# Maxima over adjacent queries, and a turned store of their negatives, in a cross-attention kernel

## The reference, cut to what matters

```
query = hidden @ Wq; keyt = enc @ Wk; valt = enc @ Wv       # 2 x 1024 queries, 2044 keys, width 640
hs = mha(query, keyt, valt)                                 # 8 heads of 80, softmax over the keys
ca_q1 = einsum('btc,th->bch', ca, Wq_ca)[:, indices, :]     # 4 tokens, 384 distinct rows
ca_hs1 = mha(ca_q1, hidden, hidden)
ca_hs2 = mha(ca_hs1 @ Wq, ca @ Wk_ca, ca @ Wv_ca)
out = (hs + ca_hs2) @ Wout + b_out + hidden
```

## Time and profile before

| what | value |
| --- | --- |
| median of the three executions | 1228.3 us |
| the profiled execution's own time | 1228.01 us |
| its span, first to last instruction | 1226.2 us |
| granted TensorE clock over the span | 1.00 |
| busy: PE, PEld | 1214.0 us, 956.8 us |
| busy: DVE, ACT, POOL | 829.0, 679.7, 205.6 us |
| PE, line 210 (maxima): count, busy | 480, 194.2 us |

### The profile page before, as it was taken

The page is one execution under the profiler, slowest core; times in us unless marked ns, Lnnn a source line. Parts: engine busy times, 40 slices in busy tenths (PEclk is TensorE's granted clock), DMA queues, the critical chain, the costliest instruction groups (busy, mean ns, idle before and its releaser), DMA issues.

```text
span 1226.2 us, 14526 instructions
## 1 busy us (share of the span) xinstructions
PE 1214.0 (99%) x5644; PEld 956.8 (78%) x5644; DVE 829.0 (68%) x1168; ACT 679.7 (55%) x773; POOL 205.6 (17%) x114
## 2 busy tenths in 40 slices
PE   7999999999999999999999999999999999999999
PEld 6889888898667677777777777777777777776899
DVE  6439825592244378888878878888888888885552
ACT  6333324222544367677677677677677677778310
POOL 1100000001000011312322222221221221221233
PEclk9999999999999999999999999999999999999999
DMA  8974795793840064154254344344345335332254
GB/s 304 350 284 165 237 344 199 265 315 94 234 115 1 1 194 97 65 151 109 80 137 108 91 126 108 104 119 111 105 112 127 95 103 146 111 91 65 69 211 150
DMA packets 80335, 180.68 MB, mean 147 GB/s; under 512 B 17305, under 2 KB 33945, under 8 KB 76138
## 3 DMA queue, kind: packets, MB, share of 16 engines
q1 hardware_dynamic: 72554, 157.33, 42.5%
q0 software_dynamic: 2816, 11.80, 3.0%
q10 hardware_dynamic: 4896, 10.62, 2.5%
HBM read 116.32 MB, written 63.24 MB: 146 GB/s over the span
## 4 chain that ended last, share of the span: by engine, by line
PE 99%; ACT 0%; DMA 0%; issue 0%; DVE 0%; ACTq 0%
PE at_ps L1232 29%; PE bank L653 20%; PE at_ps L1213 19%; PE at_ps L210 9%; PE acc_t_ps L1009 7%; PE at_ps L1419 6%; PE s_ps L976 2%; PE bank L630 2%; PE bank L600 1%; PE f_ps L949 1%; PE acc_t_ps L987 1%; PE f_ps L210 1%; PE f_ps L928 1%; PE f_ps L938 0%; DMA ctx_f<-in_ctxT 0%; PE at_ps L1422 0%
## 5 line engine op out<-in xcount | busy, mean ns | idle before, releaser
L218 DVE TENSOR_REDUCE mpart<-at_ps 128x1 f32<-128x512 f32 x480 | 326.7, 687 | 109.7 <-PE at_ps L210 108.1
L1154 ACT ACTIVATE prob_hi<-at_ps 128x1024 fp32r<-128x1024 f32 (+1 forms) x256 | 263.2, 1028 | 194.4 <-PE at_ps L1213 194.4
L1232 PE MATMUL at_ps<-prob_hi,v 128*81 128x512 f32 (+1 forms) x1024 | 318.9, 396 | 0.2 <-issue 0.2
L1091 DVE TENSOR_TENSOR prob_lo<-probs,prob_hi 128x1024 fp32r<-128x1024 f32 (+1 forms) x211 | 271.1, 1285 | 23.4 <-ACT probs L1159 23.4
L1159 ACT ACTIVATE probs<-at_ps 128x1024 f32<-128x1024 f32 (+1 forms) x256 | 261.1, 1020 | 0.0
L1232 PEld LDWEIGHTS at_ps<-prob_hi,v 128*81 128x81 f32 (+1 forms) x1024 | 153.8, 151 | 59.5 <-issue 6.1
L1091 POOL TENSOR_TENSOR prob_lo<-probs,prob_hi 128x1024 fp32r<-128x1024 f32 x45 | 108.1, 2402 | 519.7 <-ACT probs L1159 519.7
L210 PE MATMUL at_ps<-a 128*128 128x512 f32 x480 | 194.2, 405 | 0.0
L210 PEld LDWEIGHTS at_ps<-a 128*128 128x128 f32 x480 | 153.6, 320 | 32.0 <-DVE mpart L218 1.3
L1213 PE MATMUL at_ps<-a 128*128 128x512 f32 (+1 forms) x512 | 161.5, 396 | 1.2 <-ACT probs L1159 0.6
L1213 PE MATMUL at_ps<-b 113*128 113x512 f32 (+1 forms) x512 | 160.6, 394 | 0.0
(11 more groups left out here) (144 smaller groups left out, 1452.8 us busy)
## 6 DMA issues: line engine op xcount, KB each, us to landing
v_hi_d<-v_t SPq DMA_DIRECT2D x16, 648.0 KB, 6.4
v_lo_d<-v_t SPq DMA_DIRECT2D x16, 648.0 KB, 8.5
v<-v_hi_d SPq DMA_DIRECT2D x16, 648.0 KB, 4.8
v<-v_lo_d SPq DMA_DIRECT2D x16, 648.0 KB, 5.9
k_hi_d<-out_hi SPq DMA_DIRECT2D x40, 256.0 KB, 4.8
k_lo_d<-out_lo SPq DMA_DIRECT2D x40, 256.0 KB, 5.4
a<-k_hi_d SPq DMA_DIRECT2D x16, 640.0 KB, 7.3
b<-k_hi_d SPq DMA_DIRECT2D x16, 640.0 KB, 10.9
```

The costliest lines, as they stand in the source:

```text
L218: dve.tensor_reduce(self.mpart[:, g % 2, qt, c:c + 1], mx_ps[k % 2][:, 0:w], AX, ALU.max).then_inc(self.mx_done, 1)
L1091: eng.tensor_tensor(pl[n % PB][0:r, :], prob[n % PF][0:r, :], ph[n % PB][0:r, :].bitcast(F32), ALU.subtract).then_inc(sem, 1)
L1154: act.activation(ph[n % PB][0:r, :], s_ps[n % 2][0:r, :], ACT.Exp, scale=SCALE).then_inc(ph_done, 1)
L1232: mm = pe.matmul(o_ps[:, u * CH:(u + 1) * CH], a[0:r, t, :], y[n % PB][0:r, u * CH:(u + 1) * CH], start=t == 0 and m == 0, stop=t == KT - ...
```

## The change

The query tile of a step takes 128 adjacent queries, so its weights lie side by side. Partition p of the negated maxima then holds queries p, p+128, and so on. A thirty-third step per head turns them: PE multiplies the 128 x 8 negated maxima (as weights) with an identity of 128 x 128, which gives 8 rows of 128 in the PSUM buffer of the step; DVE copies them to `mrow`; SP stores the 8 rows as 8 runs of 512 bytes. `STEPS` is 33, and the buffers alternate over it. The identity is a new input, loaded once by SP in the token stage and copied once by POOL.

The new step stands in tile 12 of the head before (for head 0 in the token stage, one round behind step 31). PE has nothing between the scores there, then the new step, then the first two steps of the next head:

```diff
 NA = 3
 MXN = ST * SKV // CH
+STEPS = MXN + 1
 FIRST_PIECES = (2, 3, 2, 3, 3, 2, 3, 3, 2, 3, 3, 3)
 EARLY = 4
...
         self.mtop = sb("mtop", [P, 2, ST])
         self.mneg = sb("mneg", [P, 2, ST], F32R)
+        self.eye = sb("eye", [P, P], F32R)
+        self.mrow = sb("mrow", [ST, 2, P], F32R)
 
         self.qk_in = [sem(f"at_qk_in{r}") for r in range(NA)]
...
 
         p = g % 2
-        sp.wait_ge(self.neg_done, g + 1)
-        sp.dma_start(self.queries_b(g)[SHIFT:SHIFT + 1, :].rearrange("o (q g) -> o q g", q=P).bitcast(F32),
-                     self.mneg[:, p, :].bitcast(F32)).then_inc(self.neg_in[p], 16)
+        sp.wait_ge(self.mx_done, (g + 1) * STEPS)
+        sp.dma_start(self.queries_b(g)[SHIFT:SHIFT + 1, :].rearrange("o (t q) -> o t q", q=P).bitcast(F32),
+                     self.mrow[:, p, :].bitcast(F32)).then_inc(self.neg_in[p], 16)
 
     def score_piece(self, pe, mx_ps, g, k):
 
-        n = g * MXN + k
-        qt, c = divmod(k, SKV // CH)
-        w = min(CH, SK - c * CH)
+        n = g * STEPS + k
+        to = mx_ps[n % 2]
         if k == 0:
             self.a_loaded(pe, g)
         if n >= 2:
             pe.wait_ge(self.mx_done, n - 1)
-        pe.matmul(mx_ps[k % 2][:, 0:w], self.queries_a(g)[:, qt:SQ:ST], self.keys_a(g)[:, c * CH:c * CH + w],
-                  start=True, stop=True).then_inc(self.mx_full, 1)
+        if k < MXN:
+            qt, c = divmod(k, SKV // CH)
+            w = min(CH, SK - c * CH)
+            pe.matmul(to[:, 0:w], self.queries_a(g)[:, qt * P:(qt + 1) * P], self.keys_a(g)[:, c * CH:c * CH + w],
+                      start=True, stop=True).then_inc(self.mx_full, 1)
+        else:
+            if g == 0:
+                pe.wait_ge(self.eye_done, 1)
+            pe.wait_ge(self.neg_done, g + 1)
+            pe.matmul(to[0:ST, 0:P], self.mneg[:, g % 2, :], self.eye[:], start=True, stop=True
+                      ).then_inc(self.mx_full, 1)
 
     def max_piece(self, dve, mx_ps, g, k):
-        n = g * MXN + k
-        qt, c = divmod(k, SKV // CH)
-        w = min(CH, SK - c * CH)
+        n = g * STEPS + k
+        at = mx_ps[n % 2]
         dve.wait_ge(self.mx_full, n + 1)
-        dve.tensor_reduce(self.mpart[:, g % 2, qt, c:c + 1], mx_ps[k % 2][:, 0:w], AX, ALU.max
-                          ).then_inc(self.mx_done, 1)
+        if k < MXN:
+            qt, c = divmod(k, SKV // CH)
+            w = min(CH, SK - c * CH)
+            dve.tensor_reduce(self.mpart[:, g % 2, qt, c:c + 1], at[:, 0:w], AX, ALU.max).then_inc(self.mx_done, 1)
+        else:
+            dve.tensor_copy(self.mrow[:, g % 2, :], at[0:ST, 0:P]).then_inc(self.mx_done, 1)
 
     def top(self, dve, g):
 
         p = g % 2
-        dve.wait_ge(self.mx_done, (g + 1) * MXN)
+        dve.wait_ge(self.mx_done, g * STEPS + MXN)
         dve.tensor_reduce(self.mtop[:, p, :], self.mpart[:, p], AX, ALU.max).then_inc(self.mtop_done, 1)
         dve.wait_ge(self.mtop_done, g + 1)
...
         onehot_f = ca_f[:, 0:SQ]
         onehot = s.sb("onehot", [P, SQ], F32R)
+        eye_f = s.sb("eye_f", [P, P])
         p1 = [kept["p1_0"]] + [s.sb(f"p1_{i}", [P, 2, CD]) for i in (1, 2)]
         raw = kept["raw"]
...
 
             k -= MAX_FROM * pairs
-            return [k] if 0 <= k < MXN else []
+            return [k] if 0 <= k < STEPS else []
 
         def folded(n):
...
             written(sp)
             sp.dma_start(kept["wk2"][:], d["wk2_frame"]).then_inc(wk2_in, 16)
+            sp.dma_start(eye_f[:], d["eye"]).then_inc(eye_in, 16)
             shift_tokens(sp, kept, ca[0], 0, range(NH))
             sp.wait_ge(wk2_full, 1)
...
             pool.memset(at.one[:], 1.0).then_inc(at.one_done, 1)
             pool.wait_ge(at.one_done, 1)
+            pool.wait_ge(eye_in, 16)
+            pool.tensor_tensor(at.eye[:], eye_f[:], at.one[:].to_broadcast([P, P]), ALU.mult).then_inc(at.eye_done, 1)
             pool.wait_ge(oh_in, 16)
             pool.tensor_tensor(onehot[:], onehot_f, at.one[:].to_broadcast([P, SQ]), ALU.mult).then_inc(oh_done, 1)
...
                     token_scores(n - 1)
             pe.wait_ge(oh_done, 1)
-            pe.wait_ge(at.mx_done, MXN)
+            pe.wait_ge(at.mx_done, STEPS)
             fold_values(0, 0)
             token_scores(len(heads) - 1)
...
     g, t = divmod(n + EARLY, KT)
     each = MXN // KT
-    return [(g + 1, each * t + k) for k in range(each)] if g + 1 < G else []
+    rows = [None, (g, MXN)] if t == 0 and g < G else []
+    return rows + ([(g + 1, each * t + k) for k in range(each)] if g + 1 < G else [])
 
 
...
             for n in range(N):
                 g, t = divmod(n, KT)
-                todo = pieces(n)
-                for h, k in todo[:SPLIT_AT]:
+                todo = [piece for piece in pieces(n) if piece]
+                first = SPLIT_AT if todo and todo[0][1] < MXN else 0
+                for h, k in todo[:first]:
                     at.max_piece(dve, mx_ps, h, k)
                 split(n + 1)
-                for h, k in todo[SPLIT_AT:]:
+                for h, k in todo[first:]:
                     at.max_piece(dve, mx_ps, h, k)
                 if todo and todo[-1][1] == MXN - 1:
...
                 def between():
 
-                    if todo:
-                        at.score_piece(pe, mx_ps, *todo.pop(0))
+                    piece = todo.pop(0) if todo else None
+                    if piece:
+                        at.score_piece(pe, mx_ps, *piece)
 
                 if n == 0:
...
         "bias": b_out.reshape(1, HID), "caT": ca.transpose(2, 0, 1).reshape(CD, B * NT),
         "wqca": wqca.reshape(HID, 3 * HT), "caBD": ca_bd.reshape(B, 3 * HT, NH * CD),
-        "mask": mask.reshape(HID, NH), "wk2_frame": frame, "onehot": onehot,
+        "mask": mask.reshape(HID, NH), "wk2_frame": frame, "onehot": onehot, "eye": np.eye(P, dtype=np.float32),
     }
 
```

More of the change, by code:

```diff
@@ L119, in __init__ @@
         self.mx_full, self.mx_done = sem("at_mx_full"), sem("at_mx_done")
-        self.mtop_done, self.neg_done = sem("at_mtop"), sem("at_neg")
+        self.mtop_done, self.neg_done, self.eye_done = sem("at_mtop"), sem("at_neg"), sem("at_eye")
         self.o_raw = [spare2[0:DA, 0:SQ], spare[0:DA, 0:SQ]]
@@ L715, in tokens @@
         xn_in = [[s.sem(f"tk_xn_in{j}") for j in range(pairs)], kept["xn1_in"]]
-        oh_in, oh_done = s.sem("tk_onehot_in"), s.sem("tk_onehot")
+        oh_in, oh_done, eye_in = s.sem("tk_onehot_in"), s.sem("tk_onehot"), s.sem("tk_eye_in")
         ntop_in = kept["ntop_in"]
@@ L1403, in tensor @@
                 if n == 0:
-                    pe.wait_ge(at.mx_done, G * MXN)
+                    pe.wait_ge(at.mx_done, G * STEPS)
                 elif n < 3:
```

## The result

The changed kernel takes 1222.88 us (median of 6, 1222.38 to 1223.41) against 1228.29 us (median of 6, 1227.75 to 1228.81): a ratio of 0.9956, 95% interval 0.9944 to 0.9969. It is faster by 5.4 us, 0.44%.

The account below looks back on a forecast made before the run. The prediction took PE, busy 99% of the span, as the bound; -4.9 - 0.2 + 0.2 + 0.8 + 1.2 = -2.9 us gave 1225.4 us, range 1222.9 to 1228.6.

Parts of the forecast that it names:

- The rate of the load: Full tiles, heads 2 to 15: adjacent queries save 11 ns in each of 448 steps, 4.9 us less (4.0 to 6.7).
- The wait behind POOL's normalisation: Late maxima beside POOL's normalisation: about 55 ns of PE's gain a head ends as longer wait, 0.8 us back (0 to 1.0).
- Head 1's steps: 32 steps, mostly three to a tile: DVE bounds (3.28 us against PE's 3.02), so 0.2 us less (0 to 0.35).
- The wait at the change of heads: First value product waits for ACT; one step's 11 ns ahead only lengthens that wait: 15 times, 0.2 us back.
- The identity product: 16 more products on PE, 75 ns each: 1.2 us more (0.9 to 3.7), without waiting for the negated maxima.
- 0.2 us of room: Tile 12: PE's second step, at 744.40, comes 0.2 us after DVE's copy ends at 744.2, so the reordering costs nothing.
- The store: SP's store moves from 742.7 to 744.2, lands at 746.1, is wanted at 747.40; 1.3 us of cover, counted at nothing.
- A: Rival: the whole 15 ns step excess is the load's, nothing given back; 1222.4 us, or 1223.5 with waits; chance 0.12.
- B: Rival: spread load is hidden, the 9 to 15 ns excess is something else; only identity product left, 1229.5 us; chance 0.10.
- C: Rival: DVE's new order holds PE in tile 12, 0.26 us a head, 3.9 us in all; 1229.3 us; chance 0.09.
- D: Rival: late store makes each head's first score product wait; 12 us at 4.0 us landing time, 1237 us; chance 0.04.
- The sum's own good end: Every term of the whole sum at its good end: -6.5 us, so 1221.8 us.

Follow-up runs that it names:

- last but one experiment: Changed kernel with the second step of the first tile of heads 1 to 15 moved ahead of the value products: 1220.61 us, ratio 0.9935 to the kernel before.

## Why the prediction was wrong

*The rate of the load: right, a little small.* The full tiles without a wait gain 0.026 us each, 13 ns a step where 11 were taken; 182 such tiles give 4.7 us instead of 4.0. Adjacent queries alone give all of it. Why a load of 320 ns costs a full stream 13 ns, and one of 310 ns only 3, is not shown.

*The wait behind POOL's normalisation: this step failed.* The prediction said "about 55 ns of PE's gain a head end as a longer wait: 15 x 0.055 = 0.8 us back". The reasoning on DVE was sound: the late maximum does come later relative to PE, and the step's load is now 131 ns late where it was 63, 68 ns more for the 55 forecast. But the step was priced as if only the *product* waited, whatever its load. The load waits too: one of 320 ns makes up nothing, so that 63 ns were lost, and one of 188 ns makes up 115, so that now 16 are. Tile 10 gained 0.076 us instead of growing against the others: 14 x 0.076 = 1.1 us saved, where 0.46 us lost had been summed, an error of 1.5 us and the largest one. The two kernels with the spread load in chosen steps show it: 0.026 us without a wait, 0.125 with one. The row to read was there, the PEld row that starts at 737.56, just behind the end of the maximum.

*Head 1's steps: the same error, on a wrong bound.* The prediction's "so DVE bounds" (3.28 us against 3.02 a tile) gave 0 to 0.35 us, 0.2 taken; 0.85 us was gained. DVE was not the bound: in tiles 1 to 11 of head 0 it was busy for 29.6 of 33.5 us, as some tiles have two steps and in two of them POOL makes the low part. Most of the tiles with three steps now take 3.01 to 3.02 us, PE's own sum. What DVE does here is to finish some maxima late: 6 of the 30 loads wait for one. Such a place in the kernel before, and in the changed one:

```profile
449.76 0.31 PEld L210 LDWEIGHTS at_ps<-a 128*128 128x128 f32 x1
...
450.24 0.63 PE L1213 MATMUL at_ps<-b 113*128 113x512 f32 x2
```

```profile
450.00 0.19 PEld L215 LDWEIGHTS at_ps<-a 128*128 128x128 f32 x1 [0.16 <-DVE mpart L231]
...
450.34 0.62 PE L1233 MATMUL at_ps<-b 113*128 113x512 f32 x2
```

It is 0.48 us from the load to the next product, and now 0.34, as in tile 10. The six loads were late by 136 ns in the mean and lost all of it; they are late by 162 now and lose about 49. That is 0.5 us, and 30 steps at 13 ns are the other 0.4. The kernel with stride 4 agrees: these tiles take 33.50 us there, against 32.74 and 33.59 before. No run took the wait away here alone.

*The wait at the change of heads: right.* Tile 0 gained 0.012 us, one step of two. The last but one experiment shows what that wait was worth.

*The identity product: right.* 59 ns for its slot and 72 ns for what it adds to tile 12, for 75 taken. In heads 1 to 14 it waits for nothing, and the copy took 0.27 us for 0.25 and ended 2.44 us behind the tile's start, as forecast. The "0.2 us of room" behind it was that of the product, though. Its load comes a slot earlier and had none: it is 97 ns late, and that costs nothing only because the load is short now. This is the failed step once more, and what hid it here was luck: it was not in the reasoning. In tile 12 of head 0 the product costs 0.33 us, where DVE is late; this was not seen.

*The store: hidden, as said*, issued at 741.78 and first wanted at 744.95, where tile 14 starts. The trace gives no landing time for it, but tile 13 is as short as its neighbours, so nothing waits for it.

*The rivals.* A, the whole excess of 15 ns, gave 1222.4, or 1223.5 where the waits take a part. The result lies between these, but not by A's account: the rate was 13 ns, and the rest came from waits that gave time back instead of taking it. B, the load hidden whatever its stride, with the Trainium skill's price by columns alone ("TensorE: Matmul & The Clock Gate", "LDWEIGHTS (loading the stationary operand)"), is refuted: same columns, 188 and 320 ns, and the two spread loads in tile 5 alone cost 0.026 us. C occurred in head 0 alone, not in the steady heads. D did not occur.

In sum: -2.9 us forecast, then -0.7 for the rate, -1.5 for tile 10, -0.65 for head 1, +0.15 for tile 12 of head 0 (+0.2 where +0.05 was in the sum), which is -5.6. The two profiled executions differ by that, 1228.01 and 1222.38 us; the medians differ by 5.4. The range was too narrow because it bounded the wait from one side only, between 0 and a loss. The sum's own good end, 1221.8, would have held the result, by errors that it did not name.

## What to carry to other kernels

Where a product waits on a semaphore, see whether its weight load waits with it; then the load's length is on the path, however well loads are hidden elsewhere, and shortening it paid five times as much in such a tile here as in a full stream. Where it is shorter than the slot, it also makes up for a late start: 188 ns here made up 115, 320 ns nothing. Lay weight columns side by side; of the spacings tried, two float32 in 16 bytes is the widest that is nearly free. Before building a new step, look for a wait on another engine that an existing step can fill: moving one step to the change of heads was worth half as much as this change.

## What the hardware showed that was not expected

A weight load of 128 float32 columns takes 188, 195, 310 and 320 ns at strides of 1, 2, 4 and 8 floats. At 310 ns it costs a full stream 3 ns a product, at 320 ns 13 ns. A load that waits for a maximum starts 0.05 us behind its end. One store of 8 runs of 512 bytes holds SP for 0.66 us, one of 128 runs of 32 bytes for 0.475: fewer and longer runs were not cheaper to issue. A column of 128 elements of 4 bytes takes SP 0.6 us and lands 2.0 us after issue. Behind about 2 us without products the granted clock of PE fell in some heads, to 0.52 to 0.65 over the next 3.5 us in the five that were read, and stayed at 1.00 in four others.
